# Another order of the same operations in the ternary ("bit") feed-forward stage of a Flamingo kernel on one core

## Chip, core and metric

The kernel runs on one NeuronCore of a Trainium2 chip (the other seven are idle). The metric is the device time of one execution in microseconds (us), lower is better; the median of three runs stands for a kernel. TensorE (PE), VectorE (DVE), ScalarE (ACT), GpSimd (POOL) and SyncE (SP) are programmed by hand: each has its own list of instructions, executed in that order, and they wait for one another through semaphores only.

## What is computed

The reference is a chain of eight residual layers on x, 2048 tokens (32 x 64) of 256 values. The change touches the sixth, a feed-forward layer with quantised activations and ternary weights:

```python
def bit_linear(x, w, b):
    gamma_x = clip(max(abs(x), axis=-1), 1e-5)
    x_dq = clip(round(x * 127 / gamma_x), -128, 127) * gamma_x / 127
    gamma_w = clip(mean(abs(w)), 1e-5)
    w_dq = clip(round(w / gamma_w), -1, 1) * gamma_w
    return x_dq @ w_dq.T + b

gate = silu(bit_linear(xn, gate_w, gate_b))      # xn = layernorm(x); 256 -> 1024
val = bit_linear(xn, val_w, val_b)
x = x + tanh(g_ffn[2]) * bit_linear(gate * val, out_w, out_b)   # 1024 -> 256
```

So each token's 1024 products gate * val are scaled by their own largest magnitude, rounded, and multiplied with the last weights.

## The kernel before

**Tiling.** All of x stays in SBUF as 16 tiles of 128 tokens. A block is four tiles, so the stage has four blocks b = 0 to 3, written out one after another, not as a loop of the hardware. A tile t has two halves f of 512 hidden columns; together they are the eight steps n = 2t + f of a block.

**What each step is.**
- `gate_value(b,t,f)` (PE, L1800 and L1805): four bf16 matmuls of the gate and the value columns into banks 2(n%3) and 2(n%3)+1, and two with six rows that add the biases. It may start when `gated` has freed the banks three steps back.
- `silu(b,t,f)` (ACT, L1908): Silu of the gate bank into `bg[f]`.
- `gated(b,t,f)` (DVE, L1989): Silu times value into `bh[t%2]`; it frees both banks. It counts the semaphore `bh_ready`.
- `measure(b,t)` (DVE, L1997 to L2000): a tile's largest magnitudes (a reduction over 1024) and their reciprocals.
- `scaled(b,t)` (ACT, L1900): times the reciprocal plus 1.5 * 2^23, which rounds.
- `to_ints(b,t)` (DVE, L2007): back to small whole numbers, as bf16. This and `scaled` are the rounding.
- `turn_gated(b,t)` (PE, L1835), `turned(b,t)` (ACT, L1915): eight transposes into bank 6 and the copy out of it.
- `project(b,t)` (PE, L1846), `finish(b,t)` (DVE, L2016): the last matmul into bank 7 and its addition to x. `project(b,t)` waits until `finish` of the tile before has read.
- For the next layer norm: `tile_statistics` (DVE, L162), the merging and Newton steps `norm_step(0)` to `(10)` (DVE, tiny, for example L152 and L151), each waiting for the one before, and `normalise(..., step=2)`, four tensor_scalar of 128x256 from x to `xn` (DVE, L195). In block b they work for block b + 1; in block 3 for block 0 of the next layer.
- `ints(b+1)` on DVE (L1199 to L1211) quantises the next block's input; `turn_ints`, `turn_parts` (PE, L1817, L1825) transpose it; `ints`, `rows` on ACT (L1892, L1896) copy it.
- `add_bias(b)` (POOL, L1963): adds the last layer's bias to the block's x, one tensor_tensor of 128x1024, both inputs in SBUF. It waits for `bh_ready` 8b + 4, that is `gated(b,1,1)`, and nothing else of weight runs on POOL in the stage.

**What sets the order.** The lists in `bit_tensor`, `bit_scalar` and `bit_vector`. Work of block b - 1 (tiles 2 and 3) is mixed into block b. Two waits matter most here: `silu` of step n waits for `gated` of step n - 2 (the buffer `bg[f]`), and `gated(b,t,0)` waits for the rounding of tile t - 2 (the buffer `bh[t%2]`). After the last block, the DVE list goes on with `finish(3,0)`, two `gated`, and `early_rotate(0)` (L2193), with which the next layer's chain through POOL and a round trip through DRAM begins.

Of the kernel before, what the change touches and what calls it, by code (L numbers as in the profile page):

```python
# [67 lines left out]
def flamingo_kernel(nc, a, out):  # L68
    ctx = ExitStack()
    with ctx:  # L70
# [1214 lines left out]
        def bf_bank(i):  # L1285
            return bank[i].bitcast(BF16)
# [501 lines left out]
        def bit_tensor(pe, ph):  # L1788
# [39 lines left out]
            def turn_gated(b, t):  # L1828
                pe.wait_ge(bh_int_ready, BT * b + t + 1)
                if b > 0 or t > 0:  # L1830
                    pe.wait_ge(bh_intT_ready, BT * b + t)
                if t == 2 and b + 1 < BLOCKS:
                    pe.wait_ge(b_intT_ready, 2 * (b + 1) + 2)
                for m in range(MC):
                    ins = nc.tensor.transpose(bf_bank(6)[:, m * P:(m + 1) * P], bh_int[:, t % 2, m * P:(m + 1) * P],  # L1835
                                              ident_h[:, :])
                ins.then_inc(bh_turned, 1)
# [16 lines left out]
            for b in range(BLOCKS):  # L1854
                gate_value(b, 0, 0)
                gate_value(b, 0, 1)
                gate_value(b, 1, 0)
                gate_value(b, 1, 1)
                if b > 0:
                    turn_gated(b - 1, 2)  # L1860
                gate_value(b, 2, 0)
                if b > 0:
                    turn_gated(b - 1, 3)
                    project(b - 1, 2)
                gate_value(b, 2, 1)
                if b > 0:
                    project(b - 1, 3)
                turn_gated(b, 0)
                gate_value(b, 3, 0)
                turn_gated(b, 1)  # L1870
                gate_value(b, 3, 1)
                if b + 1 < BLOCKS:
                    turn_ints(b + 1)
                else:
                    early_project(pe, 0)
                project(b, 0)
                if b + 1 < BLOCKS:
                    turn_parts(b + 1)
                else:
                    early_project(pe, 1)  # L1880
                project(b, 1)
# [7 lines left out]
        def bit_scalar(act, link, ph):  # L1889
            def ints(b):  # L1890
                act.wait_ge(b_turned, 2 * b + 1)
                nc.scalar.activation(b_intT.rearrange("p c n -> p (c n)"), bf_bank(6), ACT.Copy).then_inc(b_intT_ready, 1)  # L1892

            def rows(b):
                act.wait_ge(b_turned, 2 * b + 2)
                nc.scalar.activation(r_rows, bf_bank(6)[0:len(SPLITS2), 0:BTOK], ACT.Copy).then_inc(b_intT_ready, 1)  # L1896

            def scaled(b, t):
                act.wait_ge(hrec_ready, BT * b + t + 1)
                nc.scalar.activation(bh[:, t % 2, :], bh[:, t % 2, :], ACT.Identity, bias=to_whole[:, 0:1],  # L1900
                                     scale=hrec[:, t:t + 1]).then_inc(h_rounded, 1)

            def silu(b, t, f):
                n = 8 * b + 2 * t + f
                if n >= 2:
                    act.wait_ge(bh_ready, n - 1)
                act.wait_ge(b_gv, n + 1)
                nc.scalar.activation(bg[:, f, :], bank[2 * ((2 * t + f) % 3)], ACT.Silu,  # L1908
                                     scale=tok_scale[:, b % 2, 0, t:t + 1]).then_inc(b_silu, 1)

            def turned(b, t):
                act.wait_ge(bh_turned, BT * b + t + 1)
                if BT * b + t >= 2:
                    act.wait_ge(b_out, BT * b + t - 1)
                nc.scalar.activation(bh_intT[:, t % 2, :, :].rearrange("p m n -> p (m n)"), bf_bank(6),  # L1915
                                     ACT.Copy).then_inc(bh_intT_ready, 1)

            ints(0)
            rows(0)
            for b in range(BLOCKS):  # L1920
                silu(b, 0, 0)
                if b > 0:
                    scaled(b - 1, 3)
                silu(b, 0, 1)
                silu(b, 1, 0)
                silu(b, 1, 1)
                if b > 0:
                    turned(b - 1, 2)
                scaled(b, 0)
                if b > 0:  # L1930
                    turned(b - 1, 3)
                scaled(b, 1)
                silu(b, 2, 0)
                turned(b, 0)
                silu(b, 2, 1)
                turned(b, 1)
                if b + 1 < BLOCKS:
                    ints(b + 1)
                silu(b, 3, 0)
                if b + 1 < BLOCKS:  # L1940
                    rows(b + 1)
                silu(b, 3, 1)
                scaled(b, 2)
            scaled(BLOCKS - 1, 3)
            turned(BLOCKS - 1, 2)
            turned(BLOCKS - 1, 3)
# [30 lines left out]
        def bit_vector(dve, link, ph):  # L1977
# [50 lines left out]
            for b in range(BLOCKS):  # L2028
                after = (b + 1) % BLOCKS
                if b > 0:  # L2030
                    finish(b - 1, 0)
                    gated(b - 1, 3, 0)
                    gated(b - 1, 3, 1)
                link.mark(tile_statistics(after))
                if b > 0:
                    to_ints(b - 1, 2)
                norm_step(link, 0)
                gated(b, 0, 0)
                norm_step(link, 1)
                if b > 0:  # L2040
                    measure(b - 1, 3)
                norm_step(link, 2)
                gated(b, 0, 1)
                norm_step(link, 3)
                measure(b, 0)
                norm_step(link, 4)
                if b > 0:
                    to_ints(b - 1, 3)
                    norm_step(link, 5)
                    finish(b - 1, 1)  # L2050
                else:
                    norm_step(link, 5)
                norm_step(link, 6)
                gated(b, 1, 0)
                norm_step(link, 7)
                gated(b, 1, 1)
                norm_step(link, 8)
                measure(b, 1)
                norm_step(link, 9)
                to_ints(b, 0)  # L2060
                norm_step(link, 10)
                if b > 0:
                    finish(b - 1, 2)
                link.hold()
                normalise(link, after, step=2)
                to_ints(b, 1)
                gated(b, 2, 0)
                if b + 1 < BLOCKS:
                    ints(b + 1)
                gated(b, 2, 1)  # L2070
                if b > 0:
                    finish(b - 1, 3)
                measure(b, 2)
# [728 lines left out]
```

## Time and profile before

| | us |
|---|---|
| median of three runs | 1497.91 (1497.61 to 1499.65) |
| the profiled execution's own time | 1499.28 |
| its span, first to last instruction | 1497.5 |
| PE busy | 1241.9 (83%) |
| DVE busy | 928.7 (62%) |
| ACT busy | 498.0 (33%) |
| POOL busy | 287.0 (19%) |

The shares are means over eight layers with different limits. The bit stage lies between about 876 and 982 us from the span's start, some 7% of the span. In the rows below an instruction's duration can overlap the start of the next on its engine, so what an instruction costs in a row of others is the distance from start to start.

### The profile page before, as it was taken

How to read it: one execution, taken by the hardware profiler on the slowest of the kernel's cores; microseconds unless marked ns; L12 is line 12 of the kernel's file. 1: busy time of each engine (PE TensorE's matmuls, PEld its weight loads, DVE VectorE, ACT ScalarE, POOL GpSimd, SP SyncE). 2: the span in 40 equal slices, each digit the busy share in tenths (PEclk: the TensorE clock that was granted, in tenths of full speed). 3: DMA queues.
4: the chain of work that ended last, by engine and by line, in shares of the span. 5: the costliest groups of instructions: out<-in, count | busy, mean ns of one | idle time of the engine just before them, and what ended most of it. 6: DMA issues, size and time to landing. Idle time of an engine off the chain costs nothing.

```text
span 1497.5 us, 19686 instructions
## 1 busy us (share of the span) xinstructions
PE 1241.9 (83%) x6750; PEld 695.1 (46%) x6750; DVE 928.7 (62%) x2249; ACT 498.0 (33%) x684; POOL 287.0 (19%) x302
## 2 busy tenths in 40 slices
PE   1127989898979999995887867758999999999998
PEld 0104444444534446663565523334555555456655
DVE  7994454545354336555999869857888888622222
ACT  3373121312111323332333225624555545521110
POOL 1220000000004330003444511144434343000000
PEclk9987999999989999997999959977999999999999
DMA  9200000002000020002111000022222223000000
GB/s 313 65 14 1 0 0 0 0 0 88 0 22 1 0 71 0 0 1 56 43 42 28 1 23 1 1 74 91 80 89 82 89 74 95 14 1 14 15 14 14
DMA packets 70851, 56.89 MB, mean 38 GB/s; under 512 B 26500, under 2 KB 63236, under 8 KB 70532
## 3 DMA queue, kind: packets, MB, share of 16 engines
q1 hardware_dynamic: 70148, 55.81, 12.3%
q8 instruction: 36, 0.59, 0.2%
q10 hardware_dynamic: 640, 0.26, 0.1%
q14 instruction: 27, 0.22, 0.0%
HBM read 41.03 MB, written 14.68 MB: 37 GB/s over the span
## 4 chain that ended last, share of the span: by engine, by line
PE 64%; issue 14%; DVE 14%; POOL 5%; ACT 2%; DMA 1%; DVEq 0%; SPq 0%; POOLq 0%; ACTq 0%
PE banks L1100 7%; PE banks L2328 7%; PE banks L717 6%; PE banks L500 5%; PE banks L496 5%; PE banks L933 4%; PE banks L1107 4%; PE banks L925 3%; PE banks L507 3%; POOL sb_work L1559 3%; PE banks L511 3%; PE banks L2293 3%; DVE sb_work L2541 2%; PE banks L1800 1%; PE banks L2314 1%
## 5 line engine op out<-in xcount | busy, mean ns | idle before, releaser
L2541 DVE TENSOR_REDUCE sb_work<-banks 128x2 f32<-128x512 f32 x256 | 164.7, 685 | 43.2 <-PE banks L2293 40.8
L2433 ACT ACTIVATE sb_work<-banks 128x1024 f32<-128x1024 f32 x128 | 130.9, 1023 | 125.8 <-PE banks L2314 125.7
L617 DVE TENSOR_TENSOR sb_work<-sb_work,banks 128x512 f32<-128x512 f32 x72 | 49.5, 688 | 116.6 <-ACT sb_work L584 116.6
L1100 PE MATMUL banks<-sb_work,sb_shelf 128*128 128x512 f32 x256 | 114.6, 593 | 0.0
L1559 POOL TENSOR_TENSOR sb_work<-sb_work,sb_consts 128x512 f32<-128x512 f32 x64 | 69.5, 1116 | 221.5 <-ACT sb_work L1503 208.9
L584 ACT ACTIVATE sb_work<-banks 128x512 f32<-128x512 f32 x72 | 42.9, 596 | 169.9 <-PE banks L496 109.4
L717 PE MATMUL banks<-sb_work,sb_ctx_nat 128*64 128x512 f32 (+15 forms) x512 | 90.0, 510 | 7.8 <-DVE sb_work L779 7.8
L500 PE MATMUL banks<-sb_work,sb_shelf 128*128 128x512 f32 (+1 forms) x192 | 85.7, 632 | 10.2 <-DVE sb_work L660 8.6
L1179 DVE TENSOR_TENSOR sb_work<-sb_work,banks 128x512 f32<-128x512 f32 x32 | 22.0, 687 | 115.8 <-ACT sb_work L1165 115.8
L1076 POOL TENSOR_TENSOR sb_late<-sb_w2n 128x1024 f32<-128x1024 f32 x10 | 22.7, 2268 | 353.1 <-DVE sb_work L771 352.4
L496 PE MATMUL banks<-sb_work,sb_shelf 128*128 128x512 f32 (+1 forms) x192 | 78.1, 594 | 0.0
L2328 PE MATMUL banks<-sb_work,sb_late 128*64 128x256 f32 x512 | 71.7, 401 | 0.3
L1100 PEld LDWEIGHTS banks<-sb_work,sb_shelf 128*128 128x128 f32 x256 | 48.8, 191 | 49.2 <-issue 47.9
L2328 PE MATMUL banks<-sb_work,sb_shelf 128*64 128x256 f32 x512 | 70.3, 396 | 0.1
L2293 PE MATMUL banks<-sb_work,sb_raw 48*128 48x256 bf16 x512 | 58.5, 287 | 8.5 <-DMA sb_work<-scratch 5.6
L1165 ACT ACTIVATE sb_work<-banks 128x512 f32<-128x512 f32 x32 | 19.1, 597 | 138.5 <-PE banks L1100 138.5
L717 PEld LDWEIGHTS banks<-sb_work,sb_ctx_nat 128*64 128x64 f32 x512 | 36.3, 135 | 60.4 <-issue 44.8
L925 PE MATMUL banks<-sb_work,sb_wgu 128*128 128x512 f16 x256 | 61.3, 386 | 2.5 <-DVE sb_work L994 2.5
L933 PE MATMUL banks<-sb_wpr,sb_work 128*128 128x256 f32 x256 | 60.1, 380 | 3.2 <-DVE sb_work L1012 3.2
L500 PEld LDWEIGHTS banks<-sb_work,sb_shelf 128*128 128x128 f32 (+1 forms) x192 | 32.0, 189 | 60.6 <-issue 37.5
L1107 PE MATMUL banks<-sb_raw,sb_work 128*128 128x256 f32 x256 | 59.8, 379 | 0.0
L1107 PEld LDWEIGHTS banks<-sb_raw,sb_work 128*128 128x128 f32 x256 | 48.4, 190 | 17.2 <-issue 12.0
(303 smaller groups left out, 2376.8 us busy)
## 6 DMA issues: line engine op xcount, KB each, us to landing
scratch<-sb_raw SPq DMA_DIRECT2D x32, 192.0 KB, 2.0
sb_raw<-scratch SPq DMA_DIRECT2D x32, 192.0 KB
sb_work<-scratch SPq DMA_DIRECT2D x32, 192.0 KB
sb_work<-ctx_t SPq DMA_DIRECT2D x8, 512.0 KB, 3.5
sb_work<-ctx_t SPq DMA_DIRECT2D x16, 256.0 KB, 4.5
scratch<-sb_raw SPq DMA_DIRECT2D x32, 128.0 KB, 1.9
sb_ctx_nat<-ctx SPq DMA_DIRECT2D x1, 2048.0 KB, 11.1
sb_raw<-wguT SPq DMA_DIRECT2D x1, 2048.0 KB, 15.4
```

The costliest lines, as they stand in the source:

```text
L496: ins = nc.tensor.matmul(dst, w[:, c, m0:m0 + ms], moe_xT[:, c, :], start=c == 0, stop=c == KC - 1, skip_group_check=True)
L500: ins = nc.tensor.matmul(dst, w[:, m0:m0 + ms], zz[:, k, :], start=False, stop=True, skip_group_check=True)
L717: ins = nc.tensor.matmul(o, ctx_nat[:, tap, g * SEQ:(g + 1) * SEQ], xg[:, g, :, l0 + 1 + 2 * tap:SEQ + 1 + 2 * tap], start=tap == TILES - ...
L925: ins = nc.tensor.matmul(bank[2 * (m % 2) + half], wgu[:, c, half * FF1 + m * P:half * FF1 + (m + 1) * P], xs[:, c, :], start=c == 0 and n ...
L933: ins = nc.tensor.matmul(bank[4 + t // 2][:, (t % 2) * DIM:(t % 2 + 1) * DIM], h1[:, m % 4, t * P:(t + 1) * P], wpr[:, m, :], start=m == 0 ...
L1100: ins = nc.tensor.matmul(bank[2 * (m % 2) + half], w[:, c, m * P:(m + 1) * P], xT3[:, c, :], start=c == 0, stop=c == KC - 1)
L1107: ins = nc.tensor.matmul(bank[4 + t // 2][:, (t % 2) * DIM:(t % 2 + 1) * DIM], h3[:, m % 4, t * P:(t + 1) * P], w2hT[:, m, :], start=m == ...
L1559: ins = nc.gpsimd.tensor_tensor(km_[:, hf, k, :, :], keys.unsqueeze(1).broadcast_to([P, 8, SEQ]), hm2.unsqueeze(2).broadcast_to([P, 8, SEQ ...
L2293: ins = nc.tensor.matmul(bank[u % 2][:, h * C3:(h + 1) * C3], qS[rows, i, 2 * hp + h, tc * P:(tc + 1) * P], kS[rows, i, 2 * hp + h, :], st ...
L2328: ins = nc.tensor.matmul(bank[6][k * SEQ:(k + 1) * SEQ, u * C3:(u + 1) * C3], vv3[j][:, sc_, 2 * k + u, a_ * VW3:(a_ + 1) * VW3], pt3[:, h ...
L2433: nc.scalar.activation(pt3[:, h % 2, :, :], o, ACT.Exp).then_inc(exp3, 1)
L2541: nc.vector.tensor_reduce(out=mx3[:, tc, k, 2 * hp:2 * hp + 2], in_=bank[u % 2].rearrange("p (h s) -> p h s", h=2), axis=AX, op=ALU.max).t ...
```

## The change

It moves calls in the three hand-written lists; no operation, buffer, size or semaphore is added or taken away. On ACT, `silu(b,0,1)` comes ahead of `scaled(b-1,3)`, `turned(b-1,2)` ahead of tile 1's Silu, and the Silu of tiles 2 and 3 move up by a place. On PE, the turns and projections of block b - 1 move with them. On DVE, `gated(b-1,3,*)` come behind the statistics, `measure(b-1,3)` and `finish(b-1,1)` move around `gated(b,0,*)`, all Newton steps come before or beside `gated(b,1,*)`, and `normalise(after, step=2)` stands right behind them, ahead of `measure(b,1)` and `to_ints(b,0)`; `to_ints(b,1)` and `ints(b+1)` come one `gated` later.

```diff
--- before.py
+++ after.py
@@ -1854,18 +1854,18 @@
             for b in range(BLOCKS):
                 gate_value(b, 0, 0)
                 gate_value(b, 0, 1)
+                if b > 0:
+                    turn_gated(b - 1, 2)
                 gate_value(b, 1, 0)
                 gate_value(b, 1, 1)
                 if b > 0:
-                    turn_gated(b - 1, 2)
+                    project(b - 1, 2)
+                    turn_gated(b - 1, 3)
                 gate_value(b, 2, 0)
-                if b > 0:
-                    turn_gated(b - 1, 3)
-                    project(b - 1, 2)
                 gate_value(b, 2, 1)
+                turn_gated(b, 0)
                 if b > 0:
                     project(b - 1, 3)
-                turn_gated(b, 0)
                 gate_value(b, 3, 0)
                 turn_gated(b, 1)
                 gate_value(b, 3, 1)
@@ -1919,27 +1919,26 @@
             rows(0)
             for b in range(BLOCKS):
                 silu(b, 0, 0)
+                silu(b, 0, 1)
                 if b > 0:
                     scaled(b - 1, 3)
-                silu(b, 0, 1)
+                    turned(b - 1, 2)
                 silu(b, 1, 0)
                 silu(b, 1, 1)
-                if b > 0:
-                    turned(b - 1, 2)
                 scaled(b, 0)
                 if b > 0:
                     turned(b - 1, 3)
+                silu(b, 2, 0)
                 scaled(b, 1)
-                silu(b, 2, 0)
+                silu(b, 2, 1)
                 turned(b, 0)
-                silu(b, 2, 1)
                 turned(b, 1)
+                silu(b, 3, 0)
                 if b + 1 < BLOCKS:
                     ints(b + 1)
-                silu(b, 3, 0)
+                silu(b, 3, 1)
                 if b + 1 < BLOCKS:
                     rows(b + 1)
-                silu(b, 3, 1)
                 scaled(b, 2)
             scaled(BLOCKS - 1, 3)
             turned(BLOCKS - 1, 2)
@@ -2029,45 +2028,46 @@
                 after = (b + 1) % BLOCKS
                 if b > 0:
                     finish(b - 1, 0)
-                    gated(b - 1, 3, 0)
-                    gated(b - 1, 3, 1)
                 link.mark(tile_statistics(after))
                 if b > 0:
+                    gated(b - 1, 3, 0)
+                norm_step(link, 0)
+                if b > 0:
                     to_ints(b - 1, 2)
-                norm_step(link, 0)
-                gated(b, 0, 0)
                 norm_step(link, 1)
                 if b > 0:
+                    gated(b - 1, 3, 1)
+                norm_step(link, 2)
+                if b > 0:
                     measure(b - 1, 3)
-                norm_step(link, 2)
-                gated(b, 0, 1)
                 norm_step(link, 3)
-                measure(b, 0)
+                gated(b, 0, 0)
                 norm_step(link, 4)
                 if b > 0:
+                    finish(b - 1, 1)
+                norm_step(link, 5)
+                gated(b, 0, 1)
+                norm_step(link, 6)
+                if b > 0:
                     to_ints(b - 1, 3)
-                    norm_step(link, 5)
-                    finish(b - 1, 1)
-                else:
-                    norm_step(link, 5)
-                norm_step(link, 6)
+                norm_step(link, 7)
+                measure(b, 0)
+                norm_step(link, 8)
                 gated(b, 1, 0)
-                norm_step(link, 7)
+                norm_step(link, 9)
                 gated(b, 1, 1)
-                norm_step(link, 8)
+                norm_step(link, 10)
+                link.hold()
+                normalise(link, after, step=2)
                 measure(b, 1)
-                norm_step(link, 9)
                 to_ints(b, 0)
-                norm_step(link, 10)
                 if b > 0:
                     finish(b - 1, 2)
-                link.hold()
-                normalise(link, after, step=2)
+                gated(b, 2, 0)
                 to_ints(b, 1)
-                gated(b, 2, 0)
+                gated(b, 2, 1)
                 if b + 1 < BLOCKS:
                     ints(b + 1)
-                gated(b, 2, 1)
                 if b > 0:
                     finish(b - 1, 3)
                 measure(b, 2)
```

## Rows read from the trace of the kernel before

**Rows 1.** Sums by block: length, busy us of PE, PEld, DVE, ACT, POOL; clock
```profile
876.87:902.90 26.03, 24.36 (x88) 7.31 (x88) 17.57 (x50) 12.93 (x16) 5.88 (x8) 0.59 0.13 34
902.90:929.08 26.18, 18.84 (x124) 8.88 (x124) 23.81 (x66) 15.25 (x19) 3.17 (x5) 1.00 0.00 1
929.08:955.27 26.19, 20.19 (x124) 9.73 (x124) 23.82 (x66) 15.27 (x19) 3.17 (x5) 0.93 0.00 1
```

**Rows 2.** The chain of waits, block 1: start, us, what
```profile
910.64 0.68 ACT sb_work L1908
...
911.34 0.75 DVE sb_work L1989
```

**Rows 3.** Order of time, blocks 1 and 3: start, us, engine, line [idle before]
```profile
907.61 1.21 DVE L1997 TENSOR_REDUCE sb_work<-sb_work 128x1 f32<-128x1024 f32 x1
...
909.49 1.24 ACT L1900 ACTIVATE sb_work<-sb_work,sb_to_whole 128x1024 f32<-128x1024 f32 x1 [2.97 <-DVE sb_work L2000]
...
963.71 0.75 DVE L1989 SCALAR_TENSOR_TENSOR sb_work<-banks,sb_tok_scale,sb_work 128x512 f32<-128x512 f32 x1 [1.81 <-ACT sb_work L1908]
```

**Rows 4.** Order of time, DVE and POOL beside add_bias, block 1
```profile
914.57 0.16 DVE L152 TENSOR_TENSOR sb_nt<-sb_nt,sb_ve 128x4 f32<-128x4 f32 x1
...
915.84 0.75 DVE L1989 SCALAR_TENSOR_TENSOR sb_work<-banks,sb_tok_scale,sb_work 128x512 f32<-128x512 f32 x1
...
916.62 1.22 DVE L1997 TENSOR_REDUCE sb_work<-sb_work 128x1 f32<-128x1024 f32 x1
916.66 2.34 POOL L1963 TENSOR_TENSOR sb_x<-sb_x,sb_late 128x1024 f32<-128x1024 f32 x1 [15.08 <-DVE sb_work L1989]
...
918.39 0.64 DVE L152 TENSOR_TENSOR sb_nt<-sb_nt,sb_ve 128x4 f32<-128x4 f32 x1
```

**Rows 5.** Order of time, L195 without and beside POOL, attention stages
```profile
728.11 0.15 DVE L151 SCALAR_TENSOR_TENSOR sb_rs<-sb_nt,sb_rs 128x4 f32<-128x4 f32 x1
728.30 1.38 DVE L195 TENSOR_SCALAR sb_xn<-sb_x,sb_mv,sb_rs 128x256 f32 x4
...
1055.38 1.87 DVE L195 TENSOR_SCALAR sb_xn<-sb_x,sb_mv,sb_rs 128x256 f32<-128x256 f32 x4
1055.46 0.67 POOL L2209 TENSOR_TENSOR sb_raw<-sb_work,sb_raw 128x256 bf16<-128x256 f32 x1
...
1130.86 0.76 DVE L195 TENSOR_SCALAR sb_xn<-sb_x,sb_mv,sb_rs 128x256 f32 x1
```

**Rows 6.** Order of time, block 1: gate_value to Silu, gated to PE, a rounding
```profile
904.39 1.03 PE L1800 MATMUL banks<-sb_late,sb_work 128*128 128x512 bf16 x4
...
905.84 0.69 ACT L1908 ACTIVATE sb_work<-banks,sb_tok_scale 128x512 f32<-128x512 f32 x1 [0.81 <-PE banks L1805]
...
905.92 0.68 DVE L2007 TENSOR_SCALAR sb_work<-sb_work 128x1024 bf16<-128x1024 f32 x1
...
912.15 1.04 PE L1800 MATMUL banks<-sb_late,sb_work 128*128 128x512 bf16 x4 [1.13 <-DVE sb_work L1989]
```

**Rows 7.** Order of time, block 0: gated(0,1,1), add_bias, norm_step(9)
```profile
890.11 0.75 DVE L1989 SCALAR_TENSOR_TENSOR sb_work<-banks,sb_tok_scale,sb_work 128x512 f32<-128x512 f32 x1 [1.78 <-ACT sb_work L1908]
...
891.01 2.34 POOL L1963 TENSOR_TENSOR sb_x<-sb_x,sb_late 128x1024 f32<-128x1024 f32 x1 [11.38 <-DVE sb_work L1989]
...
892.67 0.70 DVE L152 TENSOR_TENSOR sb_nt<-sb_nt,sb_ve 128x4 f32<-128x4 f32 x1
```

**Rows 8.** Order of time: a slow projection in block 2, end of block 3
```profile
946.43 1.87 PE L1846 MATMUL banks<-sb_late,sb_work 128*128 128x256 bf16 x8 [2.54 <-DVE sb_x L2016]
...
978.34 1.04 PE L1846 MATMUL banks<-sb_late,sb_work 128*128 128x256 bf16 x8
...
979.51 0.48 DVE L2016 SCALAR_TENSOR_TENSOR sb_x<-banks,sb_work,sb_x 128x256 f32<-128x256 f32 x1 [0.84 <-PE banks L1846]
...
981.23 0.87 DVE L2193 SCALAR_TENSOR_TENSOR sb_raw<-banks,sb_late 128x256 f32<-128x256 f32 x2
```

**Rows 9.** Sums, PE alone, 945.69 to 949.10: length, busy, granted clock
```profile
945.69:949.10 3.41, 2.67 (x17) 0.54 0.00 0
```

## The prediction, made before the changed kernel was run

> **What bounds the kernel now.** I read the sums by block first, then the chain of waits, then the order of time on VectorE (DVE) inside one block. The sums [rows 1] cut the bit stage at the DVE instruction that starts `finish(b,0)`: blocks 1 and 2 take 26.18 and 26.19 us, and DVE is busy 23.8 us of each; TensorE (PE) 18.8 to 20.2, ScalarE (ACT) 15.3. So DVE sets the pace, and a block can give back at most the 2.4 us in which DVE does nothing useful. The chain shows where one part lies: in block 1 it leaves DVE once, goes through the Silu of tile 0, half 1 on ACT, and returns with `gated(1,0,1)` [rows 2]. The order of time says why: that Silu stands behind `scaled(0,3)`, which waits for `measure(0,3)` to end on DVE and runs from 909.49 until the Silu starts at 910.64, so DVE idles 1.81 us [rows 2, 3]. The same 1.81 us stands in all of blocks 1 to 3; the last is in [rows 3]. The second part is hidden in a duration. The Newton step `norm_step(9)`, a 4-element product (L152), takes 0.64 us where the same instruction elsewhere takes 0.16 [rows 4]. It starts while GpSimd (POOL) runs `add_bias` (L1963, 2.34 us from 916.66) and ends with it: DVE was held 0.48 us, until 916.66 + 2.21 = 918.87. The reduction at 916.62, beside the same POOL instruction, is not held: 1.22 us for the 1.21 in [rows 3]. Work alone is then 26.18 - 1.81 - 0.48 = 23.89 us per block.
>
> **The change, part by part.** No instruction is added or removed; all durations stay.
>
> 1. *Both Silu of tile 0 in front of `scaled(b-1,3)`, and `measure(b-1,3)` earlier than `gated(b,0,0)` and `finish(b-1,1)`.* From `finish(b-1,0)` as time 0, by the DVE times from start to start in block 1 (0.39 a `finish`, 1.31 the statistics, 0.67 a `gated`, 0.60 a rounding, 1.77 a `measure`; some 0.07 less than a printed duration, as L1989 and L2007 in [rows 4, 6]), `gated(b-1,3,1)` starts at 3.4, so PE may start gate_value(b,0,1) at 4.2 (0.81 from the `gated` at 911.34 to PE), ACT starts its Silu 1.45 later, at 5.7 (904.39 to 905.84, [rows 6]), and it is done at 6.4. `gated(b,0,1)` comes up at 7.2: no wait. `scaled(b-1,3)` follows at 6.3 and is done at 7.6; its rounding comes up at 7.9. `scaled(b,0)`, `scaled(b,1)` and the other Silu have 0.4 us or more in hand. Price: -1.81 us in each of blocks 1 to 3. The cover is thin (0.35 us at the rounding of tile 3); between nothing and all of the 1.81 I take all, and leave the rest to the range.
>
> 2. *`gated(b-1,3,0)` and `(3,1)` behind the statistics.* They free the banks of the next gate_value, so PE starts (b,0,0) 1.0 us later than now. PE has 5 to 7 us of room in a block [rows 1]: 0.
>
> 3. *`norm_step(9)` out of the shadow of `add_bias`.* Now all Newton steps come before it. Price: -0.48 us a block.
>
> 4. *`normalise(after, step=2)`, four 128x256 tensor_scalar (L195), directly behind `gated(b,1,1)`.* This is the step that decides. `gated(b,1,1)` is what releases `add_bias`: POOL starts 0.82 us after it starts [rows 4]. In the new order DVE does `norm_step(10)` 0.67 after it and is ready for L195 another 0.19 later, as L151 to L195 in [rows 5]: at 0.86, when POOL has begun. Does L195 need what POOL holds? The bit stage never shows the two side by side. The attention stage does: four L195 take 1.38 us alone [rows 5], but 1.87 when a POOL tensor_tensor of 0.67 us started at 1055.46, and later, at 1130.86, a single one takes 0.76 against 0.40. In the first case POOL had started 0.08 us after DVE, and still came first. Hence, as for L152, L195 waits until `add_bias` lets go, 2.21 us after its start: 0.82 + 2.21 - 0.86 = 2.17 us of standing DVE in each block. Should the first L195 win, the second is held instead (as at 1130.86), for the same sum. Ends: 0 (L195 is not held) to 2.25. I take 2.17, since the nearest row is the very same instruction.
> Rates alone speak for the other end: L195 takes 0.34 us for 256 elements, where the rounding L2007 does 1024 in 0.60 to 0.68 [rows 5, 6]. The Trainium skill ("VectorE: DVE Perf Modes", the table of the TRN2 errata) gives 58 plus the elements, divided by the mode's factor, in cycles at 0.96 GHz: 0.33 us at one result a cycle, 0.19 at two. And "SBUF — State Buffer", "Who interferes with whom", says that an instruction with one SBUF input contends with GpSimd only in a mode that uses both ports. By the two together L195 would not be held, the time that the first rival gives; the stretched rows are against that.
>
> 5. *`measure(b,1)`, `to_ints(b,0)` behind `normalise`.* They feed turn_gated(b,0). It now comes 18.0 us after time 0, 4.5 us after PE ends gate_value(b,2,1). In blocks 1 and 2 PE is then done with gate_value(b,3,1) at 22.9, and `turn_ints` waits for DVE until 24.0: covered, with 1.1 us in hand. In block 3, without `ints`, it is not: turn_gated(3,0) comes about where it is now, but project(2,3), which now stands ahead of it, comes behind it (0.87). The tail's project(3,0), now at 978.34, and `finish(3,0)`, which already waits 0.84 us for it, move by +0.7 [rows 8].
>
> **Block sums.** Blocks 1 and 2: -1.81 - 0.48 + 2.17 = -0.12 each. Block 0 has no Silu wait of this kind: TensorE is at half clock (0.59 over the block) and bounds it up to `gated(0,1,1)` at 890.11, which stays. From there the new DVE order takes 14.3 us to `finish(0,0)` against 12.8: +2.25 held at L195 (POOL starts 0.90 behind here), -0.54 not held at L152 [rows 7], -0.2 for Newton steps that moved ahead: +1.5. Block 3: +0.7.
>
> The clock. After 2.54 us of idle PE, at 946.43, the eight matmuls of a projection take 1.87 us where they take 1.04 at 978.34; the granted clock over these 3.41 us is 0.54, the level of 1.2 GHz instead of 2.4, and PE works 2.67 of them [rows 8, 9]. Half of that work time, less what was begun earlier, is lost: 1.2 us. Block 1, in the same order of work, keeps its clock (1.00, [rows 1]). The idle before turn_gated(b,0) grows to 4.5 us, so I take this loss every time: covered in blocks 1 and 2 by the 1.1 us, open in block 3: +1.2. In block 0, PE newly stands 1.8 us before turn_gated(0,0), just when the clock rises: +0.3 by estimate (0 if it rises as now, +2.8 if it stays low through gate_value(0,3,1)).
>
> Sum: 1.5 + 0.3 - 0.12 - 0.12 + 0.7 + 1.2 = +3.5 us. From `finish(3,0)` on the order is the old one: two `gated`, `early_rotate(0)` at 981.23, GpSimd's split, the DMAs [rows 8], so a shift passes through. Against the profiled execution (span 1497.5, its own time 1499.28, which is 1.4 above the median) that gives 1502.8; against the median of the runs, 1497.91, it gives **1501.4 us**, +0.23%. A measurement of this kernel can tell about 0.2%, 3.0 us, from no change.
>
> **Rivals.**
> - *L195 is not held (faster).* Place: the four tensor_scalar behind `gated(b,1,1)`; it decides if the hold is below about 1 us a block. Then a block takes 23.89, -2.29 twice; block 0 -0.75, block 3 -1.4 (PE's turn_gated(3,0) is 2.2 us earlier): -6.8, **1491.1**. For it: the rate of L195. Against: 1055.38 and 1130.86. Chance 0.13.
> - *DVE wins and keeps what it has over all four L195; POOL waits.* Then `add_bias` starts 1.3 us late, a `measure` hides most of it, and the rounding `to_ints(b,0)` is held about 0.45 us: -1.84 twice, -0.3, -1.0: -5.0, **1492.9**. Against: at 1130.86 POOL got in between two L195. Chance 0.08.
> - *The low clock lasts.* PE idles more, and in block 0 at the rise. If it stays at half through the first gate_value of block 1 (2.8 us each for 1.5), `finish(0,0)` is 2.5 later again and `gated(1,0,1)` waits 1.3: +7.5, **1505.4**. Chance 0.06.
> - *The forecast:* the Silu wait goes, a hold of the same size comes. Chance 0.73; its own range 1498.4 to 1505.0, for the clock terms (0 to +2.8 and 0 to +1.2) and the thin cover of step 1; 0.46 of it lies above 3.0 us, 0.27 within.
>
> That the change does not do what it says is hardly possible: the lists are the order issued. Range: from 1490.5, to hold the first rival, to 1505.0. Faster 0.21, same 0.27, slower 0.52.
>
> **What would show it.** Right: no idle before L1989 in block 1; one L195 per block, or L195's group, longer by 2.2 us beside L1963; L152 at 0.16; DVE's busy sum of block 1 near 26, block time 26.1; PE idle of 4 to 5 us before a L1835. Wrong: L195's group at 1.4 us beside L1963 (first rival), L1963 starting more than 2 us behind `gated(b,1,1)` (second), or gate_value at 2.8 us apart in block 1 (third). A Silu wait that is still there would mean that step 1 was mis-timed.

## The result, and the profile after

The changed kernel is slower: a median of 1503.76 us over 20 runs (1498.99 to 1510.25), against 1499.26 us over 20 runs of before (1494.06 to 1502.64); the ratio is 1.0035, with a 95% interval of 1.0023 to 1.0047, that is +5.2 us (3.4 to 7.0). The prediction said 1501.4 us and +3.5. The profiled execution of the changed kernel took 1505.36 us, with a span of 1503.6.

Because a line fell out of one list, line numbers after it are one lower: `gated` is L1988, `measure` L1996, `to_ints` L2006, `finish` L2015, `add_bias` L1962. L195, L151 and L152 are as before.

The sums by block of the changed kernel, cut in the same way as [rows 1] (the first from the start of `gated(0,1,1)`, the others from `finish(b,0)` to the next; columns: length, busy us and instructions of PE, PEld, DVE, ACT, POOL, granted clock):

```profile
887.99:904.91 16.92, 15.31 (x59) 5.84 (x58) 13.84 (x28) 7.71 (x9) 3.17 (x5) 0.50 0.13 36
904.91:931.14 26.23, 20.92 (x124) 9.76 (x121) 25.42 (x65) 14.42 (x18) 3.18 (x5) 0.84 0.00 1
931.14:957.86 26.72, 21.03 (x124) 9.76 (x124) 25.41 (x66) 15.04 (x20) 3.17 (x5) 0.87 0.01 1
957.86:988.58 30.72, 25.17 (x122) 12.00 (x123) 21.93 (x55) 15.88 (x20) 2.34 (x1) 0.78 0.00 1
```

Blocks 1 and 2, 26.18 and 26.19 us in [rows 1], take 26.23 and 26.72. So what the new order gains there it loses there. The whole difference lies at the two ends: block 0 from `gated(0,1,1)` on takes 16.92 us for 12.79, block 3 takes 30.72 for 24.24. Together the four blocks are 11.2 us longer, twice the 5.2 by which the medians differ; experiment 6 comes back to that. And the granted clock, 1.00 and 0.93 in blocks 1 and 2 of [rows 1], is 0.84 and 0.87. Block 3 of before, in the same columns:

```profile
955.27:979.51 24.24, 20.16 (x118) 10.21 (x119) 20.42 (x57) 15.49 (x19) 2.34 (x1) 0.93 0.00 1
```

The order of time in block 1 of the changed kernel, which answers to [rows 3] and [rows 4]:

```profile
913.18 1.52 ACT L1908 ACTIVATE sb_work<-banks,sb_tok_scale 128x512 f32<-128x512 f32 x2
...
916.03 0.15 DVE L152 TENSOR_TENSOR sb_nt<-sb_nt,sb_ve 128x4 f32<-128x4 f32 x1
916.09 0.74 DVE L1988 SCALAR_TENSOR_TENSOR sb_work<-banks,sb_tok_scale,sb_work 128x512 f32<-128x512 f32 x1
...
916.76 0.15 DVE L151 SCALAR_TENSOR_TENSOR sb_rs<-sb_nt,sb_rs 128x4 f32<-128x4 f32 x1
...
916.91 2.35 POOL L1962 TENSOR_TENSOR sb_x<-sb_x,sb_late 128x1024 f32<-128x1024 f32 x1 [15.29 <-DVE sb_work L1988]
916.94 3.44 DVE L195 TENSOR_SCALAR sb_xn<-sb_x,sb_mv,sb_rs 128x256 f32<-128x256 f32 x4
...
920.30 1.21 DVE L1996 TENSOR_REDUCE sb_work<-sb_work 128x1 f32<-128x1024 f32 x1
...
922.06 0.68 DVE L2006 TENSOR_SCALAR sb_work<-sb_work 128x1024 bf16<-128x1024 f32 x1
...
922.80 1.03 PE L1835 MATMUL banks<-sb_ident_h,sb_work 128*128 128x128 bf16 x8 [4.34 <-DVE sb_work L2006]
```

The Silu wait is gone: no `gated` of blocks 1 to 3 has an idle time in front of it. L152, held to 0.64 us in [rows 4], takes 0.15. In their place stands the group of four L195, 3.44 us instead of 1.37, beside `add_bias`, which had started 0.03 us earlier. That it is one instruction which is held, and not all four that are slower, shows in the view of the line (durations in ns: least, median, most):

```profile
L195 DVE TENSOR_SCALAR sb_xn<-sb_x,sb_mv,sb_rs x4: 400/401/2470, 916.9 to 920.0; 128x256 f32<-128x256 f32 x4
```

2470 ns against 400: the hold is 2.07 us. The last row of the stretch above shows what follows: `turn_gated(1,0)` on TensorE comes after 4.34 us of idle time, and its eight transposes take 1.03 us where they took about 0.61 before.

What that does in block 3 is seen in the chain of waits (start, us, what), and in the `finish(3,0)` that ends the block:

```profile
975.75 1.03 PE banks L1835 x8
976.78 1.71 PE banks L1846 x8
978.49 1.71 PE banks L1800 x4
...
986.79 1.67 PE banks L1846 x8
```

```profile
988.58 0.48 DVE L2015 SCALAR_TENSOR_TENSOR sb_x<-banks,sb_work,sb_x 128x256 f32<-128x256 f32 x1 [7.74 <-PE banks L1846]
```

From `turn_gated(3,0)` on the chain runs through TensorE alone, at half clock (granted clock 0.50 from 975.75 to 988.08, busy all the time), and VectorE waits 7.74 us for it where it waited 0.84 us in [rows 8].

### The profile page after: what moved, and what is told of

Read it like the earlier page. It is cut to its first block, busy times and chain, and to the rows that moved or that the text cites. A ratio compares the mean times of both kernels' runs of the same rounds, so it can differ in the third digit from the quotient of the medians.

```text
span 1503.6 us, 19686 instructions
## 1 busy us (share of the span) xinstructions
PE 1245.8 (83%) x6750; PEld 698.0 (46%) x6750; DVE 937.6 (62%) x2249; ACT 497.6 (33%) x684; POOL 287.5 (19%) x302
## 4 chain that ended last, share of the span: by engine, by line
PE 65%; DVE 15%; issue 13%; POOL 4%; ACT 1%; DMA 1%; DVEq 0%; SPq 0%; POOLq 0%; ACTq 0%
PE banks L1100 7%; PE banks L2328 7%; PE banks L717 6%; PE banks L496 5%; PE banks L500 5%; PE banks L933 4%; PE banks L1107 4%; PE banks L925 3%; PE banks L507 3%; PE banks L511 3%; PE banks L2293 3%; POOL sb_work L1559 2%; DVE sb_xn L195 2%; DVE sb_work L2541 1%; PE banks L2314 1%
## 5 line engine op out<-in xcount | busy, mean ns | idle before, releaser
L500 PE MATMUL banks<-sb_work,sb_shelf 128*128 128x512 f32 (+1 forms) x192 | 82.2, 612 | 10.2 <-DVE sb_work L660 8.6
L496 PE MATMUL banks<-sb_work,sb_shelf 128*128 128x512 f32 (+1 forms) x192 | 78.1, 594 | 0.0
L2204 POOL TENSOR_TENSOR sb_raw<-sb_raw 128x256 f32<-128x256 f32 x32 | 23.6, 737 | 175.6 <-DVE sb_raw L2193 174.5
```

Source lines behind the costliest of these rows:

```text
L496: ins = nc.tensor.matmul(dst, w[:, c, m0:m0 + ms], moe_xT[:, c, :], start=c == 0, stop=c == KC - 1, skip_group_check=True)
L500: ins = nc.tensor.matmul(dst, w[:, m0:m0 + ms], zz[:, k, :], start=False, stop=True, skip_group_check=True)
```

## The experiments

**Theory**: two costs, one behind the other. `add_bias` holds L195 (and so VectorE) for 2.1 us a block, which takes back the Silu wait and the hold of L152; and through the longer idle time of TensorE it lowers its clock, which costs at the ends of the stage, where TensorE sets the pace. **Rivals**: the new order is itself slower, whatever POOL does; or the clock costs nothing, since VectorE covers it.

### 1. A small addition on POOL, in both orders

The addition covers 8 of each 256 columns; this kernel leaves out most of the last layer's bias.

```diff
-                xs = x[:, bass.ds(BT * b, BT), :]
-                nc.gpsimd.tensor_tensor(xs, xs, ob_b.unsqueeze(1).broadcast_to([P, BT, DIM]),
+                xs = x[:, bass.ds(BT * b, BT), 0:8]
+                nc.gpsimd.tensor_tensor(xs, xs, ob_b[:, 0:8].unsqueeze(1).broadcast_to([P, BT, 8]),
```

In the changed order:

> The changed order, but add_bias adds only 8 of each 256 columns (128x32 instead of 128x1024), so the output lacks most of the last layer's bias. Theory 'hold' (L195 stands behind the POOL addition, and the longer idle time of TensorE lowers its clock): the L195 group takes 1.4 to 1.6 us instead of 3.44, a full block about 24.0 us instead of 26.2, TensorE's idle time before turn_gated(b,0) shrinks from 4.3 to about 2.3 us, and the kernel is 8 to 13 us faster than the changed one, 5 to 8 us faster than before. Rival 'order' (the new order itself is slower, whatever POOL does): L195 stays near 3.4 us or the block near 26 us, time near the changed kernel's.

Measured: 1490.92 us, ratio to before 0.9932 (0.9907 to 0.9957). The order of time in its block 1, and its sums by block (blocks 0, 1 and 3):

```profile
913.24 0.75 DVE L1988 SCALAR_TENSOR_TENSOR sb_work<-banks,sb_tok_scale,sb_work 128x512 f32<-128x512 f32 x1
...
914.07 0.25 POOL L1962 TENSOR_TENSOR sb_x<-sb_x,sb_late 128x32 f32<-128x32 f32 x1 [15.71 <-DVE sb_work L1988]
914.10 1.38 DVE L195 TENSOR_SCALAR sb_xn<-sb_x,sb_mv,sb_rs 128x256 f32<-128x256 f32 x4
...
915.39 1.22 DVE L1996 TENSOR_REDUCE sb_work<-sb_work 128x1 f32<-128x1024 f32 x1
```

```profile
886.82:902.06 15.24, 15.02 (x58) 5.83 (x58) 11.74 (x29) 7.82 (x9) 1.08 (x5) 0.50 0.13 39
902.06:925.97 23.91, 20.82 (x122) 9.84 (x121) 23.32 (x66) 14.43 (x18) 1.08 (x5) 0.88 0.00 1
...
949.87:974.29 24.42, 20.64 (x120) 10.37 (x123) 19.90 (x57) 15.77 (x20) 0.25 (x1) 0.93 0.00 1
```

L195 takes 1.38 us again, in the same place of the same order, beside a POOL instruction of 0.25 us, and a full block takes 23.91 us where the prediction's count of pure work was 23.89. Against the changed kernel's ratio of 1.0035 that is 1.0%, some 15 us, more than the 8 to 13 expected; and 10 us below before, where 5 to 8 were expected. TensorE's idle time before `turn_gated(1,0)` is 2.29 us, and block 3 takes 24.42 us for 30.72: so this edit takes away the hold and, with the shorter idle time, most of the low clock too. The rival that blames the order falls: nothing in the order was touched.

In the order of before:

> The order of before with the same small add_bias (output lacks most of the last layer's bias). Theory 'hold': only L152 was held there, 0.48 us a block: a block takes 25.7 instead of 26.2, the Silu wait of 1.81 us stays, in all 1.5 to 2 us faster than before. Rival: if the addition weighs on more than the held instruction (memory traffic, the queue), more than 3 us faster.

Measured: 1494.4 us, ratio 0.9969 (0.9950 to 0.9988), the sums of its blocks 0 and 2:

```profile
885.66:900.90 15.24, 15.02 (x58) 5.83 (x58) 11.91 (x30) 7.13 (x8) 1.08 (x5) 0.50 0.13 40
927.36:953.08 25.72, 20.33 (x122) 9.83 (x124) 23.35 (x67) 15.28 (x19) 1.08 (x5) 0.93 0.01 1
```

Block 2 is 0.47 us shorter than the 26.19 of [rows 1], just the hold of L152. The time fell by 0.31%, 4.6 us, more than the 1.5 to 2 expected; the interval reaches down to 1.8 us. More than 3 us was the sign set for the rival, that the addition weighs on more than the held instruction. The blocks don't show that: block 3 too is 0.49 us shorter, and block 1 took 26.46 us at a clock of 0.89. The rest stays open, and experiment 6 shows that it is not peculiar to this kernel.

### 2. normalise moved out of the shadow of add_bias

```diff
                 norm_step(link, 10)
+                measure(b, 1)
+                if b > 0:
+                    finish(b - 1, 2)
+                to_ints(b, 0)
                 link.hold()
                 normalise(link, after, step=2)
-                measure(b, 1)
-                to_ints(b, 0)
-                if b > 0:
-                    finish(b - 1, 2)
```

> The changed order with normalise moved behind measure(b,1), finish(b-1,2) and to_ints(b,0); everything computed. Theory 'hold': the reduction and the finish run beside the POOL addition unhindered, to_ints is held 0.1 us or not at all, L195 not: L195 group 1.38 us, a full block 23.9 to 24.0 us, 6 to 8 us faster than before (and a little better than with the small addition, since turn_gated(b,0) comes 1.3 us earlier). Rival 'order': near the changed kernel's time, 3 us or more slower than before.

Measured: 1488.74 us, ratio 0.9927 (0.9902 to 0.9952): about 11 us faster than before (6 to 8 expected), with everything computed. It beats both kernels. The order of time in its block 1, and its sums for blocks 1 to 3:

```profile
913.13 1.22 DVE L1996 TENSOR_REDUCE sb_work<-sb_work 128x1 f32<-128x1024 f32 x1
...
913.18 2.35 POOL L1962 TENSOR_TENSOR sb_x<-sb_x,sb_late 128x1024 f32<-128x1024 f32 x1 [15.38 <-DVE sb_work L1988]
...
914.90 0.47 DVE L2015 SCALAR_TENSOR_TENSOR sb_x<-banks,sb_work,sb_x 128x256 f32<-128x256 f32 x1
...
915.29 0.78 DVE L2006 TENSOR_SCALAR sb_work<-sb_work 128x1024 bf16<-128x1024 f32 x1
916.00 1.37 DVE L195 TENSOR_SCALAR sb_xn<-sb_x,sb_mv,sb_rs 128x256 f32<-128x256 f32 x4
```

```profile
901.17:926.95 25.78, 23.70 (x125) 10.70 (x125) 23.43 (x66) 15.13 (x18) 3.19 (x5) 0.76 0.00 1
926.95:950.85 23.90, 18.67 (x126) 8.88 (x125) 23.35 (x65) 14.89 (x18) 3.19 (x5) 0.99 0.01 1
950.85:972.72 21.87, 18.77 (x120) 9.25 (x120) 19.86 (x56) 15.46 (x19) 2.35 (x1) 1.00 0.00 1
```

The same `add_bias` of 2.35 us now runs beside a reduction (1.22 us, not held) and a `finish` (0.47, not held). The rounding L2006, which does 1024 elements in 0.68 us when alone, meets the last 0.1 us of it and takes 0.78; then come the L195, 1.37. Block 2 is 23.90 us, and block 3, 30.72 in the changed kernel, is 21.87 at a clock of 1.00. Block 1 is 25.78: there the clock was low for a part (0.76), and `finish(1,0)` waited 1.80 us for TensorE.

### 3. The clock alone

Sixteen extra matmuls fill TensorE's idle time, in blocks 1 to 3:

```diff
                 gate_value(b, 2, 1)
+                if b > 0:
+                    pe.wait_ge(bh_ready, 8 * b + 4)
+                for k in range(16 if b > 0 else 0):
+                    nc.tensor.matmul(bank[0], b_intT[:, 0, 0:P], gwT[:, 0, 0, 0:512], start=True, stop=True)
                 turn_gated(b, 0)
```

> The changed order, with 16 extra 128x512 matmuls into the free bank 0 in blocks 1 to 3, in TensorE's idle time ahead of turn_gated(b,0) (3.4 us at full clock; the bank is overwritten by the next start=True). Theory 'hold' with clock: L195 still takes 3.4 us and a full block 26.1 us, but the clock stays at 1.00 in the blocks, finish(3,0) no longer waits 7.7 us but 1 to 2 us, and the kernel is 3 to 6 us faster than the changed one, within 3 us of before. Rival 'clock costs nothing' (everything is covered by VectorE): no difference to the changed kernel.

Measured: 1497.56 us, ratio 0.9992 (0.9973 to 1.0011). The sums of blocks 2 and 3, and two rows of TensorE in block 3:

```profile
928.63:954.56 25.93, 21.94 (x141) 10.29 (x141) 25.34 (x66) 15.05 (x19) 3.19 (x5) 1.00 0.00 1
954.56:979.39 24.83, 22.53 (x136) 10.76 (x136) 21.86 (x56) 15.40 (x19) 2.35 (x1) 1.00 0.00 1
```

```profile
972.46 0.62 PE L1835 MATMUL banks<-sb_ident_h,sb_work 128*128 128x128 bf16 x8 [0.80 <-DVE sb_work L2010]
...
978.22 1.04 PE L1846 MATMUL banks<-sb_late,sb_work 128*128 128x256 bf16 x8
```

L195 is still held (3.45 us), and `finish(3,0)` waits 2.53 us (1 to 2 expected). But the clock is 1.00, and from `turn_gated(3,0)` to the start of `project(3,0)` TensorE needs 5.8 us (972.46 to 978.22), where the changed kernel needs 10.8 (975.75 to 986.59 in its order of time). Block 3 is 24.83 us, the 24.2 of before plus the 0.6 or 0.7 that the prediction gave to the swapped project. Doing 48 useless matmuls made the kernel 0.43% faster, some 6 us; the profiled blocks 1 to 3 are shorter by 0.30, 0.79 and 5.89, in all 7.0 us. That is the price of the low clock in blocks 1 to 3; block 0 got no extra work and takes 16.92 us as before it. The rival that the clock costs nothing falls. What is left, hold against Silu wait, comes to about nothing in blocks 1 and 2: 25.93 us each for 26.18 and 26.19, -0.25 where -0.12 was predicted.

### 4. The Silu edit alone, and taken back

In the order of before, only this on ScalarE:

```diff
                 silu(b, 0, 0)
+                silu(b, 0, 1)
                 if b > 0:
                     scaled(b - 1, 3)
-                silu(b, 0, 1)
```

> The order of before with one edit on ScalarE: both Silu of tile 0 in front of scaled(b-1,3). Theory 'hold' (the change's first part is a gain, its L195 part takes it back): the Silu wait of 1.81 us in blocks 1 to 3 goes to nothing, L152 is still held 0.48 us, a full block takes 24.4 us, and the kernel is 4.5 to 6 us faster than before. Rival: the Silu wait is only moved (another wait of 1 us or more on VectorE takes its place, the chain lies elsewhere): a block stays above 25.5 us, less than 3 us faster.

Measured: 1493.24 us, ratio 0.9972 (0.9953 to 0.9990), the sums of blocks 2 and 3 and the held L152:

```profile
927.02:951.30 24.28, 19.80 (x122) 9.69 (x124) 23.73 (x66) 15.06 (x19) 3.18 (x5) 0.93 0.00 1
951.30:979.61 28.31, 24.52 (x116) 11.94 (x119) 20.34 (x56) 15.70 (x19) 2.34 (x1) 0.76 0.00 1
```

```profile
940.61 0.64 DVE L152 TENSOR_TENSOR sb_nt<-sb_nt,sb_ve 128x4 f32<-128x4 f32 x1
```

Block 2 is 24.28 us, 1.91 less than in [rows 1]: the Silu wait was real and goes away with this edit alone, while L152 stays held. The whole kernel gained 4.2 us, a little less than the 4.5 to 6 expected. But the profiled execution doesn't show where: in it the clock fell in block 3 (0.76), which took 28.31 us for 24.24, block 0 took 15.25 for 12.79 and block 1 24.99 for 26.18, so that the four blocks together are 3.4 us longer than in before.

In the changed order, the reverse (`scaled(b-1,3)` again in front of `silu(b,0,1)`):

> The changed order with scaled(b-1,3) back in front of silu(b,0,1) on ScalarE. By the walk of the prediction scaled(b-1,3) then runs 6.0 to 7.2 us after finish(b-1,0) and the Silu is done at 7.9, where gated(b,0,1) comes up at 7.2: a wait of 0.7 us on VectorE, a full block 0.7 us longer than the changed one (26.9), 1 to 3 us slower than the changed kernel. Rival: the longer hold of L195 covers it, no difference to the changed kernel.

Measured: 1504.76 us, ratio 1.0037 (1.0022 to 1.0051), no different from the changed kernel's 1.0035. The wait appears as the walk of the prediction has it (0.7 expected):

```profile
937.34 0.75 DVE L1989 SCALAR_TENSOR_TENSOR sb_work<-banks,sb_tok_scale,sb_work 128x512 f32<-128x512 f32 x1 [0.62 <-ACT sb_work L1908]
```

But block 2 does not grow: it takes 26.63 us, for 26.72 in the changed kernel. There `finish(2,0)` already waits 0.71 us for TensorE, and now it doesn't; the 0.62 us are covered by that. The other blocks differ more, and by the clock: block 1 took 30.45 us for 26.23, since TensorE worked at half clock to its end (0.50 from 917.9 to 929.3) and `finish(1,0)` had to wait, and block 3 took 27.19 for 30.72.

```profile
929.42 0.48 DVE L2016 SCALAR_TENSOR_TENSOR sb_x<-banks,sb_work,sb_x 128x256 f32<-128x256 f32 x1 [3.74 <-PE banks L1846]
```

So the expectation of 1 to 3 us was wrong. In block 2 the cause is that TensorE is as late as VectorE; for the whole kernel one profile can't say what evens out what.

### 5. The swap on TensorE taken back

```diff
                 gate_value(b, 2, 1)
-                turn_gated(b, 0)
                 if b > 0:
                     project(b - 1, 3)
+                turn_gated(b, 0)
```

> The changed order with project(b-1,3) back in front of turn_gated(b,0) on TensorE, as before. The prediction put 0.7 us of block 3 on this swap at full clock. Both still wait for VectorE behind the held L195, so TensorE's idle time stays above 4 us and its clock low: blocks 1 and 2 as in the changed kernel, block 3 shorter by 0 to 1.5 us; in all within 1.5 us of the changed kernel. Rival 'order on TensorE' (the swap is what costs): 3 us or more faster than the changed kernel.

Measured: 1501.24 us, ratio 1.0026 (1.0014 to 1.0039), 1.3 us less than the changed kernel, with intervals that overlap. Block 3 in its profiled execution:

```profile
952.03:979.49 27.46, 21.14 (x120) 10.45 (x123) 21.93 (x56) 15.89 (x20) 2.34 (x1) 0.88 0.00 1
```

It is 3.3 us shorter than the changed kernel's 30.72, with a clock of 0.88 for 0.78; how much of this is the swap and how much the clock can't be told from one look. By the medians the swap is not what costs most: its rival wanted 3 us or more.

### 6. Second looks at both kernels

> The changed kernel once more, for a second look at the parts that differ from one execution to another. L195 again 3.4 us in all four blocks, full blocks 26.1 to 26.8 us; where the clock is low differs: block 3 between 25 us (clock up again after 3 to 7 us) and 31 us (as in the first look).

> The kernel before once more, for a second look. In the first look the clock rose 7.8 us after gated(0,1,1) starts and finish(0,0) came 12.8 us after it; in most looks of the other kernels it rose some 18 us after, and finish(0,0) waited 2.4 to 2.9 us for TensorE. If that early rise was chance, it comes here after about 15.2 us. Full blocks 26.2 us again, each with a Silu wait of 1.81 us; block 3 24.2 to 26 us.

> A third look at the kernel before: as the second. If finish(0,0) comes 12.8 us after gated(0,1,1) in this one or in the second, the early rise is no rarity.

The changed kernel again (1511.1 us), blocks 0 and 3, then before again (1496.23 us), blocks 0, 2 and 3:

```profile
890.72:907.64 16.92, 15.09 (x58) 5.81 (x58) 13.83 (x28) 7.71 (x9) 3.17 (x5) 0.50 0.12 36
...
960.56:991.27 30.71, 24.88 (x120) 12.01 (x123) 21.93 (x55) 15.88 (x20) 2.35 (x1) 0.78 0.00 1
```

```profile
887.26:900.05 12.79, 12.26 (x60) 4.57 (x58) 12.37 (x30) 7.29 (x9) 3.19 (x5) 0.69 0.15 47
...
926.24:952.43 26.19, 20.19 (x124) 9.69 (x124) 23.82 (x66) 15.28 (x19) 3.18 (x5) 0.93 0.01 1
952.43:976.68 24.25, 20.14 (x118) 10.16 (x119) 20.44 (x57) 15.50 (x19) 2.34 (x1) 0.93 0.00 1
```

The third look at before (1497.69 us) has 12.80, 26.19, 26.19 and 24.25. So neither the 12.8 us of before nor the 30.7 of after is a single accident, and the expectation that block 0 of before would usually take 15.2 us was wrong: it took 12.8 three times out of three. Other kernels whose L195 is not held there took 15.2 (both kernels of experiment 1, those of experiment 2 and of the Silu edit alone, the first of experiment 7) or 12.4 (the second of experiment 7). The kernel of the Silu edit alone has in block 0 the very order of before, and took 15.25 at a clock of 0.50; so the low clock of block 0 comes without the new order too. All five looks with the held L195 in block 0 took 16.92.

From `gated(0,1,1)` to `early_rotate(0)` the two looks at the changed kernel show 102.3 us, the three at before 91.1: 11.2 us, twice what the medians differ by. The first look is close to the median (1505.36 against 1503.76), so that slow looks alone don't explain it. The other kernels show the same gap. The four blocks from `gated(0,1,1)` to `finish(3,0)` in the profiled execution, the difference from before's 89.4, and the difference of the whole kernel by its ratio, all in us:

| | four blocks | from before | whole kernel |
|---|---|---|---|
| changed kernel | 100.6 | +11.2 | +5.2 |
| its Silu edit taken back | 101.2 | +11.8 | +5.5 |
| its swap taken back | 97.2 | +7.8 | +3.9 |
| 16 matmuls more a block | 93.6 | +4.2 | -1.2 |
| Silu edit alone | 92.8 | +3.4 | -4.2 |
| small addition, order of before | 91.2 | +1.8 | -4.6 |
| small addition, changed order | 87.5 | -1.9 | -10.2 |
| normalise behind the rounding | 86.8 | -2.6 | -10.9 |
| small addition and 8 matmuls (7) | 85.7 | -3.7 | -6.1 |
| normalise behind, and 8 matmuls (7) | 82.3 | -7.1 | -6.6 |

Against before, the whole kernel comes out 4 to 8 us better than its blocks in eight of the ten. Against the changed kernel, blocks and whole agree within 2.4 us for all but the two kernels with 8 matmuls (3.6 and 6.5). Outside these blocks all kernels have the same instructions, in the same order but for a few in front of `gated(0,1,1)`, yet that part took 1405.0 to 1408.1 us in the three looks at before, 1403.0 and 1408.8 in the two at the changed kernel, and 1396.7 to 1406.4 in the others. So it may be that this part runs slower in before (though 1408.8 and 1406.4 us stand against that), or that its unprofiled executions have longer blocks than its three profiled ones; no run tells which. So comparisons with the changed kernel rest on blocks and times both; those with before rest on the times, and some 6 us of them are not explained.

### 7. Both costs taken away, and the candidate with filler

The small addition with 8 extra matmuls in blocks 1 to 3:

> The changed order with both suspected costs taken away: the small add_bias (output lacks most of the last layer's bias) and 8 extra 128x512 matmuls ahead of turn_gated(b,0) in blocks 1 to 3. Theory (hold and clock add up): L195 1.38 us, full blocks 23.9 us, clock 1.00 through block 3, block 3 about 22.5 us instead of 24.4, 1 to 3 us faster than the small addition alone. Rival (block 3 is set by something else than the clock): block 3 stays at 24.4 us.

Measured: 1492.55 us, ratio 0.9959 (0.9941 to 0.9976). The profiled execution does what was expected, block 3 being 22.76 us for 24.42 at a clock of 1.00:

```profile
949.15:971.91 22.76, 20.90 (x130) 9.96 (x128) 19.79 (x56) 15.40 (x19) 0.25 (x1) 1.00 0.00 1
```

The times don't: the ratio is higher than the 0.9932 of the small addition alone, though their intervals overlap. So the gain of 1 to 3 us was not found.

The candidate of experiment 2 with the same 8 matmuls:

> The candidate (normalise behind the rounding, everything computed) with 8 extra matmuls ahead of turn_gated(b,0) in blocks 1 to 3. If the clock still costs something there, it is 0.5 to 3 us faster than the candidate, with blocks of 23.9 us and block 3 near 21.9; if its shorter idle time already keeps the clock, there is no difference, or up to 1 us slower, since the extra work stands in turn_gated's way.

Measured: 1490.64 us, ratio 0.9956 (0.9936 to 0.9975): no gain over the candidate's 0.9927, again with overlapping intervals. Its profiled execution had the early rise of the clock in block 0, as before:

```profile
888.22:900.62 12.40, 11.93 (x56) 4.34 (x54) 12.05 (x28) 7.23 (x9) 3.18 (x5) 0.68 0.17 48
```

In the profiled executions the four blocks are 4.5 us shorter than the candidate's (block 0 12.40 for 15.25, block 1 23.92 for 25.78), but the times don't follow. Why, no run shows; block 1 of the candidate, with a clock of 0.76, did leave something to win.

## Why the prediction was right, and where it was not

- *What bounds the kernel.* Right: 26.18 us were 23.89 of work and two stalls. With the stalls taken away one by one, blocks of 25.72, 24.28 and 23.9 us appeared.
- *Step 1, the Silu.* Right: -1.91 us in block 2 of the Silu edit alone (1.81 predicted), and 0.62 us of wait when taken back (0.7 by the walk).
- *Step 2 and step 3.* Right: no new wait for the later `gated(b-1,3,*)` in VectorE; L152 at 0.15 us.
- *Step 4, L195 behind `gated(b,1,1)`.* Right, and it decided: held 2.07 us (2.17 predicted), POOL starting first by 0.03 us (0.04 predicted). The first rival (L195 is not held, 1491.1 us) is what the small addition makes real; that 1490.92 us came out is in part luck, since by the ratio this is 10.2 us below before and the rival had 6.8. The stretched rows from another stage were a better guide than L195's rate of 0.33 us for 256 elements. By the Trainium skill ("SBUF — State Buffer", "Who interferes with whom") an instruction with one SBUF input is held only in a mode that uses both ports. L195 was held (2.47 us for 0.40), so the trace agrees if L195 ran in such a mode, which its rate does not suggest; in which it ran, no run shows. The second rival (VectorE keeps what POOL needs over all four) fell with the same rows.
- *Step 5, the late turn_gated(b,0).* Right in its time: 17.9 us after `finish(0,0)` (922.80 - 904.91; 18.0 predicted), after 4.34 us of idle TensorE (4.5).
- *Block sums.* Blocks 1 and 2: -0.12 predicted, +0.05 and +0.53 measured. The 1.1 us said to be in hand on TensorE were not enough: at low clock VectorE waited 0.23 and 0.71 us for its projection. Block 3 without the clock: +0.7 predicted, +0.6 in the filled kernel. Block 0 at like clock: +1.5 predicted; 16.92 against the 15.25 of the Silu edit alone, +1.7.
- *"The clock."* This is the term that was mis-sized. It was right that a low clock follows the idle time before turn_gated; the prediction took one stretch like that of [rows 9], 3.41 us, and so +1.2 in block 3, nothing in blocks 1 and 2, and +0.3 in block 0. In block 3 the low level lasted through the whole of TensorE's chain: the stretch that needs 5.8 us at full clock took 10.8, and the block was 6.5 us longer, not 1.9. The filled kernel prices the clock in blocks 1 to 3 at some 6 us by the times, 7.0 by the blocks, where the sum had 1.2. In block 0 the clock was low until 18 us after `gated(0,1,1)`, not 8, which is 2.4 us, near the +2.8 that the prediction gave as the bound for this case. Whether the new order causes that is not shown: the same code took 15.25 and 12.79 us there. The third rival, that the low clock lasts, was nearer than its price and chance said, though in other places: not in the first gate_value of block 1, but at both ends. (Its terms, 3.5, 2.5 and 1.3, add to 7.3 and not 7.5.)
- *The total.* The terms forecast for the stage add to +3.5 us, and the profiled stage grew by 11.2: +2.3 more than forecast in block 0, +0.8 in blocks 1 and 2, +4.6 in block 3. That the kernel as a whole came out at +5.2 is owed to some 6 us that no term of the prediction had and that experiment 6 leaves open. The closeness of 1501.4 to 1503.76 is in part luck.

Together: the mechanism and its sign were right, a hold of L195 in place of the Silu wait and a clock that pays for it. The clock term was too small by some 5 us in blocks 1 to 3, and an unexplained difference against before hid a good part of that.

## What to carry to other kernels

Before moving an instruction to a place where another engine is triggered, look at what that trigger starts and which of the two engines' instructions exclude each other; here a reduction (1.22 us) and a PSUM-reading `finish` (0.47 us) could stand beside GpSimd's addition, and a tensor_scalar (2.47 us for 0.40), a rounding (0.78 for 0.68) and even a four-element product (0.64 for 0.15) could not. When VectorE is late, TensorE's clock can pay for it a second time, and the bill comes where TensorE is the bound: mostly in the last block here, but once in block 1. So for an upper bound count the low clock to the end of TensorE's next uninterrupted chain, not for one stretch of a trace. A stall that has two causes is best priced by taking one away at a time, with the order left alone. And add up the profiled blocks and set the sum against the medians: where the two don't meet, a good match of the total proves little.

## What was not expected of the hardware

- In block 0 of the changed kernel the first L195 started at 888.84, 0.04 us before `add_bias` at 888.88, and still was the one to wait, 2.53 us:

```profile
888.84 2.53 DVE L195 TENSOR_SCALAR sb_xn<-sb_x,sb_mv,sb_rs 128x256 f32<-128x256 f32 x1
```

- The same exclusion acts on a memset. Three instructions of the layer norm on four elements a partition, the first of them a tensor_scalar, took 1.96 to 2.10 us beside a POOL memset and ended together, so it was one hold (it cost nothing here, since VectorE had to wait for the first Silu anyway):

```profile
875.22 2.10 DVE L172 TENSOR_SCALAR sb_mv<-sb_mv 128x4 f32<-128x4 f32 x1
875.26 2.03 POOL L2238 MEMSET sb_shelf<- 128x2304 f32 x1
```

- The clock stayed at 0.50 through all of block 0's 16.92 us, with TensorE busy for 15.1 and 15.3 of them in the two looks, and in the three looks at before it rose 10 us earlier after the same work up to `gated(0,1,1)`. What decides that was not found. The order is not enough: the Silu edit alone leaves block 0 as in before (15.25 us against 12.79), and the two kernels with normalise behind the rounding have the same block 0 and took 15.25 and 12.40.
- Nor does the idle time alone decide how long the clock stays low. After 2.54 us of idle TensorE in before the granted clock was 0.54 over 3.41 us [rows 8, 9] and 0.98 over the 6.17 us behind; after 2.51 us in the kernel of the Silu edit alone it was 0.50 over 13.6 us (966.00 to 979.60), with TensorE busy for 12.9 of them.
